# One order for every chunk of ScalarE and GpSimd, group means a chunk earlier, and other places for loads, stores and input statistics

## The chip, the cores and the metric

The kernel runs on one core of a Trainium2 chip. Its five engines run side by side and meet only at semaphores: TensorE (PE in the profile), VectorE (DVE), ScalarE (ACT), GpSimd (POOL), and SyncE (SP), which here only issues DMAs. The metric is the device time of one execution in microseconds (us). Three runs of the kernel before took 4111.73, 4111.97 and 4114.0 us; the median is 4111.97.

## The reference

x has 16 images of 512 channels and 64 x 64 pixels, fp32. Cut to what matters:

```python
# layer 0
g = group_norm(x)                                  # 32 groups of 16 channels, over 16 x 64 x 64 values
gs = [sum_c(g * shift(g, di, dj)) for di in -2..2 for dj in -2..2]     # 25 local correlations
gs = gs / sqrt(sum(gs * gs) + 1e-6)
y = x + relu(W @ concat(g, gs) + bias)             # 1x1 convolution, 537 -> 512
# layer 1
v = group_norm(y)
s = relu(w2 @ relu(w1 @ mean_hw(v) + b1) + b2)     # one number for each image and channel
q = clip(floor(s), 0, 5)
out = y + (s - q) * maxpool[q + 1](v) + (q + 1 - s) * maxpool[q](v) + v   # pools of 1, 3, ..., 13
```

## The kernel before, in words

The program has two phases. The first, some 2500 us long, makes y; the second takes each plane (one channel of one image) of y from memory and pools it. The change touches the first phase alone.

**Tiling.** An image is kept in SBUF as 128 partitions x 4 channel tiles x 4096 pixels, in one of two halves of the arena by the parity of its number. It is worked on in eight chunks of eight rows (512 pixels), numbered 0 to 7 here as in the code, so that "the fourth chunk" is c = 3. `STATS_AT` is 4. Images are numbered 0 to 15. Image 0, image 14 and image 15 are written out in the program; images 1 to 13 are passes of a hardware loop (`Fori`) on VectorE and SyncE (on GpSimd and ScalarE the loop goes to 14; TensorE's holds seven images and runs twice).

**What one chunk costs each engine, in its order:**

- TensorE: `picks` (L1245, gathers the correlations of this chunk from the masked products), two `gram` steps of the next chunk (L1198, products of pixel pairs), `tail` (L1278, the descriptor's part of the convolution of the previous chunk), `norm` (L1268), the two other `gram` steps, then four convolution outputs (L1221 to L1223, 48 matmuls) with `turn_blocks` (L1259) after the first. PSUM banks 4 and 5 hold the gram products in turn: gram step 2 can start only when VectorE has masked step 0.
- VectorE: four `mask` instructions (L791), one for each gram step, with `descriptor` (L833, L837) after the second, `y_stats` (L803, statistics of y for layer 1: the first output after the third mask, three after the fourth), and `wide_rows` (L812 to L827, six maxima of each pixel with its neighbours in the row, of the chunk before). `x_stats` (L741, four instructions) takes the statistics of one chunk of a coming image. In most chunks it stands ahead of the masks.
- ScalarE: `normalise` (L580, L582) of the chunk three ahead, Square (L613), Sqrt (L617), four `conv_out` (L594), `after` (L601).
- GpSimd: `low_parts` (L438, the rounding rest of the fp16 numbers), `residual` (L447, adds the convolution to x in place), `halves` (L457, L459).
- SyncE: `regroup` (12 DMAs of 8 KB that lay the descriptor out for `tail`), `store_wide` (1 MB, the maxima), `store` (2 MB, a quarter image of y), `load` (2 MB, a quarter of the image two ahead, once the same quarter of y is stored).

A chunk of an engine that waits holds up all that is behind it in its queue.

**Group means.** Once per image, the statistics of all eight chunks of the next image are put together: `group_sums` (L751, four instructions on VectorE), `group_average` (L1286, a TensorE matmul into bank N), `group_spreads` (L758 to L764), `group_spread` (L1290, a matmul), `group_root` (L565, ScalarE), `group_values` (L769 to L781). All of these are in chunk 4. TensorE issues `group_spread` last in that chunk; VectorE comes to `group_spreads` only after the maxima. Since the scale is there only at the chunk's end, ScalarE and GpSimd take chunk 5 in another order than all others (`soon`): everything of the coming image's chunk 0 stands behind `conv_out` and `residual`.

```python
if c == STATS_AT and not last and n == 0:      # TensorE, L1315
    group_average(i + 1)
if c == STATS_AT and not last:                 # TensorE, L1317
    group_spread(i + 1)
if c < 5 and left >= 1:                        # VectorE, L862: ahead of the masks
    x_stats(i + 1, c + 2 if c < 4 else CH - 1)
```

At the end of the phase, SyncE stores the last quarter of y and then the maxima of chunks 6 and 7. `wide_rows` of a chunk waits at L819 until the maxima of the chunk before have been stored, since there is one buffer for them.

## Time and profile before

| | |
|---|---|
| median of three runs | 4111.97 us |
| profiled execution, its own time | 4115.68 us |
| its span | 4113.9 us |
| mean granted TensorE clock | 0.915 |
| PE busy | 3403.6 us (83%) |
| DVE busy | 3392.5 us (82%) |
| ACT busy | 1971.2 us (48%) |
| POOL busy | 2080.1 us (51%) |
| packets' time, queue q1 (all of SyncE's DMAs) | 29.2% of 16 engines |

The span begins with the first instruction and ends with the last; the execution's own time is 1.8 us longer. The view of slices cuts the span into 40 equal parts of 102.8 us; a digit 9 is a part in which the engine is busy for 90% or more. In rows of single instructions, or of runs of like ones, the first number is the start, the second the duration, both in us; in brackets stands how long the engine was idle just before and what ended that. "issue" means that nothing the profile shows was waited for. Where the text says "+4.7", it means 4.7 us after the chunk's first `picks` matmul (L1245) on TensorE, which is taken as the start of the chunk.

### The profile page before, as it was taken

The numbers are of one execution on the slowest core, as the hardware profiler recorded it, in microseconds if no ns is written. First come the engines' busy times: TensorE is split into PE (matmuls) and PEld (weight loads), VectorE is DVE, ScalarE is ACT, GpSimd is POOL, SyncE is SP. The second block draws the span as 40 slices with busy tenths as digits, with TensorE's granted clock in tenths as the row PEclk, the third lists the DMA queues.
The fourth block names the chain that finished last, engine by engine and source line by source line (L and its number), as shares of the span: only waits on it lengthen the run. The fifth ranks groups of instructions, "written<-read, shape, count | busy, mean of one in ns | idle before, by whom it ended". The sixth has DMA issues, their size and how long they took to land. (4 is left out here: it accounts for less than half of the span.)

```text
span 4113.9 us, 83924 instructions
## 1 busy us (share of the span) xinstructions
PE 3403.6 (83%) x28232; PEld 1926.1 (47%) x28233; DVE 3392.5 (82%) x3619; ACT 1971.2 (48%) x3219; POOL 2080.1 (51%) x1564
## 2 busy tenths in 40 slices
PE   5999999999999999999999996465666666877665
PEld 3665665565655655665655664122222222333222
DVE  6877777777777777777777766899999999999997
ACT  4544545545545545445545540334444445554566
POOL 4555555555546546556555551345455544454443
PEclk9999999999999999999999996677888888998888
DMA  5454444454445445454454334464565666864466
GB/s 194 162 187 162 167 173 171 169 176 165 160 168 183 160 172 179 161 175 175 167 175 169 129 121 85 172 235 182 226 246 229 265 257 236 338 271 169 182 250 242
DMA packets 251672, 782.36 MB, mean 190 GB/s; under 512 B 97433, under 2 KB 97433, under 8 KB 229273
## 3 DMA queue, kind: packets, MB, share of 16 engines
q1 hardware_dynamic: 219600, 417.47, 29.2%
q0 software_dynamic: 31568, 358.89, 22.2%
q8 instruction: 228, 3.74, 0.4%
q14 instruction: 276, 2.26, 0.2%
HBM read 421.55 MB, written 409.08 MB: 202 GB/s over the span
## 5 line engine op out<-in xcount | busy, mean ns | idle before, releaser
L1041 DVE TENSOR_TENSOR arena<-arena 128x2048 f32<-128x2048 f32 (+8 forms) x635 | 1454.8, 2319 | 57.2 <-DMA arena<-wide_planes,arena 13.8
L438 POOL TENSOR_TENSOR arena<-arena 128x512 f16<-128x512 f32 x512 | 652.4, 1279 | 883.8 <-ACT arena L582 883.5
L1395 PE MATMUL psum<-arena 128*128 128x512 f32 x896 | 532.8, 680 | 465.2 <-issue 313.7
L1198 PE MATMUL psum<-arena 128*128 128x256 f16 (+1 forms) x6344 | 731.1, 274 | 81.5 <-DVE arena L791 61.0
L1221 PE MATMUL psum<-arena 128*128 128x512 f16 x2048 | 777.3, 380 | 1.0 <-ACT arena L594 1.0
L1222 PE MATMUL psum<-arena 128*128 128x512 f16 x2048 | 777.0, 379 | 0.0
L1223 PE MATMUL psum<-arena 128*128 128x512 f16 x2048 | 776.9, 379 | 0.0
L447 POOL TENSOR_TENSOR arena<-arena 128x512 f32 (+1 forms) x512 | 639.6, 1270 | 226.6 <-ACT arena L594 221.7
L580 ACT ACTIVATE arena<-arena,gbias,grstd 128x512 f32 (+1 forms) x512 | 413.7, 808 | 637.3 <-PE psum L1223 527.6
L1198 PEld LDWEIGHTS psum<-arena 128*128 128x128 f16 x6344 | 597.4, 100 | 175.2 <-DVE arena L791 68.5
L1397 PE MATMUL psum<-arena 128*128 128x512 f32 x1072 | 601.6, 659 | 57.0 <-ACT psum L667 47.9
L681 ACT ACTIVATE arena<-psum 128x512 f32<-128x512 f32 x536 | 314.2, 599 | 689.6 <-PE psum L1397 680.4
L803 DVE BATCH_NORM_STATS2 bny<-arena 128x6 f32 (+1 forms) x512 | 351.4, 690 | 266.6 <-POOL arena L447 262.1
L530 POOL DMA_INDIRECT out<-arena x67 | 183.9, 2745 | 747.3 <-issue 747.3
L1395 PEld LDWEIGHTS psum<-arena 128*128 128x128 f32 x896 | 188.4, 217 | 725.2 <-issue 546.3
L594 ACT ACTIVATE arena<-psum,bias_sb 128x512 f32<-128x512 f32 x512 | 337.2, 684 | 219.7 <-POOL arena L447 207.4
L582 ACT ACTIVATE arena<-arena,gbias,grstd 128x512 f16 (+1 forms) x512 | 409.4, 800 | 0.0
L667 ACT ACTIVATE psum<-arena 128x512 f32<-128x512 f32 x536 | 383.1, 766 | 48.6 <-ACT arena L681 47.5
L1397 PEld LDWEIGHTS psum<-arena 128*128 128x128 f32 x1072 | 230.2, 216 | 371.3 <-issue 307.8
L791 DVE TENSOR_TENSOR arena<-psum,cst 128x256 f32<-128x256 f32 x496 | 280.6, 589 | 108.4 <-PE psum L1198 108.3
L741 DVE BATCH_NORM_STATS2 bnx<-arena 128x6 f32 (+1 forms) x512 | 315.1, 680 | 29.5 <-issue 20.7
L1223 PEld LDWEIGHTS psum<-arena 128*128 128x128 f16 x2048 | 200.3, 98 | 241.9 <-issue 0.3
(151 smaller groups left out, 3085.8 us busy)
## 6 DMA issues: line engine op xcount, KB each, us to landing
arena<-in_x SPq DMA_DIRECT2D x64, 2048.0 KB, 13.2
wide_planes<-arena SPq DMA_DIRECT2D x128, 1024.0 KB, 9.3
y_planes<-arena SPq DMA_DIRECT2D x64, 2048.0 KB, 7.8
arena<-arena SPq DMA_DIRECT2D x1536, 8.0 KB, 1.8
arena<-wide_planes,arena POOLq DMA_INDIRECT x69, 11.6
arena<-plane_records,arena POOLq DMA_INDIRECT x67, 7.7
arena<-y_planes,arena POOLq DMA_INDIRECT x67, 9.8
out<-arena POOLq DMA_INDIRECT x67, 9.2
```

Of the source, the lines that this page charges most:

```text
L438: pool.tensor_tensor(gl[:, ct, slot], g32[:, ct % 2, :], gh[:, ct, slot], ALU.subtract).then_inc(s_gl, 1)
L447: pool.tensor_tensor(y, y, relu[:, o % 2, :], ALU.add).then_inc(s_added, 1)
L580: act.activation(g32[:, ct % 2, :], piece, ACT.Identity, bias=gbias[:, ct:ct + 1], scale=grstd[:, ct:ct + 1])
L582: act.activation(gh[:, ct, (c % RING) * CW:(c % RING + 1) * CW], piece, ACT.Identity, bias=gbias[:, ct:ct + 1], scale=grstd[:, ct:ct + 1]) ...
L667: act.activation(psum[:, b, :], bufs[:, u, b * CW:(b + 1) * CW], ACT.Identity, bias=recs_in[:, u, 3:4], scale=recs_in[:, u, 0:1]).then_inc ...
L1041: ins = dve.tensor_tensor(dst, a, b, ALU.max)
L1198: return pe.matmul(dst, w, m, start=(k == 0), stop=(k == nk - 1))
L1221: pe.matmul(dst, h, gh[:, ct, slot], start=(ct == 0), stop=False)
L1222: pe.matmul(dst, h, gl[:, ct, slot], start=False, stop=False)
L1223: last = pe.matmul(dst, l, gh[:, ct, slot], start=False, stop=(ct == CT - 1))
L1395: pe.matmul(dst, diag[:, s, 0, :], small[:, s, b * ROWS:(b + 1) * ROWS, 1:W + 1], start=False, stop=False, skip_group_check=True)
L1397: pe.matmul(dst, diag[:, s, 1, :], big[:, s, b * CW:(b + 1) * CW], start=False, stop=True, skip_group_check=True).then_inc(s_mix, 1)
```

## The change

- VectorE: `x_stats` moves from before the masks to behind the fourth mask, ahead of the last three `y_stats`, by a new function `coming`. Its chunks are other ones: each of chunks 0 to 3 takes one chunk (4 to 7) of the next image, chunk 4 none, chunks 5 and 6 one each (0, 1) and chunk 7 two (2, 3) of the image after.
- Group means: `group_sums` goes to the end of chunk 3 and `group_average` behind its convolutions; `group_spreads` stands at the start of chunk 4, ahead of the masks; `group_spread` behind the second convolution output of chunk 4; `group_values` behind its y statistics, ahead of the maxima.
- TensorE gets waits with which bank N is not written too early: `norm` of chunk 4 waits for the copy of the means (L758 before), `group_spread` for `after` of chunk 5.
- ScalarE and GpSimd take every chunk in one order (`soon` goes).
- SyncE: a chunk is `regroup`, then in odd chunks `load`, then `store_wide` of the chunk before, then in even chunks `store`. Loads go in chunks 3, 5, 7 and in chunk 1 of the next image (before: 4, 6, and 0 and 1 of the next). After the last image the maxima are stored ahead of y.

```diff
@@ SyncE
-            def image(i, prev=True, load_prev=True, load_own=True):
+            def image(i, first=False, left=2):
                 for c in range(CH):
-                    if c >= 2:
-                        store_wide(i, c - 2)
-                    elif prev:
-                        store_wide(i - 1, CH + c - 2)
                     regroup(i, c)
-                    if c == 0 and prev:
-                        store(i - 1, 3)
+                    if c >= 3 and c % 2 and left >= 2:
+                        load(i, c // 2 - 1)
+                    if c == 1 and not first and left >= 1:
+                        load(i - 1, 3)
+                    if c:
+                        store_wide(i, c - 1)
+                    elif not first:
+                        store_wide(i - 1, CH - 1)
                     if c % 2 == 0 and c:
                         store(i, c // 2 - 1)
-                    if c < 2 and load_prev:
-                        load(i - 1, 2 + c)
-                    if c in (4, 6) and load_own:
-                        load(i, c // 2 - 2)
+                    elif c == 0 and not first:
+                        store(i - 1, 3)
...
+            store_wide(B - 1, CH - 1)
             store(B - 1, 3)
-            for c in (CH - 2, CH - 1):
-                store_wide(B - 1, c)
@@ ScalarE (GpSimd likewise)
-                    soon = ahead and c + 3 != CH
-                    if soon:
+                    if ahead:
                         normalise(*ahead, cts=(0, 1), first=first)
...
-                    if ahead and not soon:
-                        normalise(*ahead, cts=(0, 1))
...
-                        normalise(*ahead, cts=(3,) if soon else (2, 3))
+                        normalise(*ahead, cts=(3,))
@@ VectorE
+            def coming(i, c, first, left):
+                todo = []
+                if first and c < 2:
+                    todo += [(1, 2 * c), (1, 2 * c + 1)]
+                if c < 4 and left >= 1:
+                    todo += [(i + 1, c + 4)]
+                if c > 4 and left >= 2:
+                    todo += [(i + 2, c - 5)]
+                if c == CH - 1 and left >= 2:
+                    todo += [(i + 2, 3)]
+                return [lambda at=at: x_stats(*at) for at in todo]
...
-                    sums = [lambda: group_sums(i + 1)] if c == STATS_AT and not last else []
-                    between = [[], sums + [lambda: descriptor(i, c)], res[0:1], res[1:4]]
...
+                    between = [[], [lambda: descriptor(i, c)], res[0:1], coming(i, c, first, left) + res[1:4]]
+                    if c == STATS_AT and not last:
+                        group_spreads(i + 1)
...
+                    if c == STATS_AT - 1 and not last:
+                        group_sums(i + 1)
+                    if c == STATS_AT and not last:
+                        group_values(i + 1)
@@ TensorE
             def norm(i, c, last):
+                if c == STATS_AT and not last:
+                    pe.wait_ge(s_vchain, (i + 1) * STATS_CHAIN + 2)
...
                         if c == STATS_AT and not last and n == 0:
-                            group_average(i + 1)
-                    if c == STATS_AT and not last:
-                        group_spread(i + 1)
+                            group_spread(i + 1)
+                    if c == STATS_AT - 1 and not last:
+                        group_average(i + 1)
```

Three places of the instruction order show what this does. First VectorE at the start of image 14 (chunk 0), where the code is written out; before:

```order
567 L741 BN_STATS bnx<-arena 128x6 x4
568 L791 TENSOR_TENSOR arena<-psum,cst 128x2x16x8 x2
569 L833 RECIPROCAL arena<-arena 128x128
570 L837 TENSOR_TENSOR arena<-psum,arena 128x128
571 L791 TENSOR_TENSOR arena<-psum,cst 128x2x16x8
572 L803 BN_STATS bny<-arena 128x6
573 L791 TENSOR_TENSOR arena<-psum,cst 128x2x16x8
574 L803 BN_STATS bny<-arena 128x6 x3
```

And now (lines of VectorE's helpers have smaller numbers by six: L785 is the mask, L735 `x_stats`, L797 `y_stats`):

```order
565 L785 TENSOR_TENSOR arena<-psum,cst 128x2x16x8 x2
566 L827 RECIPROCAL arena<-arena 128x128
567 L831 TENSOR_TENSOR arena<-psum,arena 128x128
568 L785 TENSOR_TENSOR arena<-psum,cst 128x2x16x8
569 L797 BN_STATS bny<-arena 128x6
570 L785 TENSOR_TENSOR arena<-psum,cst 128x2x16x8
571 L735 BN_STATS bnx<-arena 128x6 x4
572 L797 BN_STATS bny<-arena 128x6 x3
```

The four input statistics stood ahead of the first mask and now stand behind the fourth.

Second, VectorE from the end of chunk 3 to the masks of chunk 4 of the same image, now:

```order
616 L797 BN_STATS bny<-arena 128x6 x3
617 L745 BN_AGGR aggx<-bnx 128x2 x4
618 L806 TENSOR_TENSOR arena<-arena 128x32x31
...
623 L821 TENSOR_TENSOR arena<-arena 128x32x31
624 L752 COPY gm<-psum 128x4
625 L754 TENSOR_TENSOR gd<-aggx,gm 128x4
626 L756 TENSOR_TENSOR gd<-gd 128x4
627 L758 TENSOR_TENSOR gd<-gd,aggx 128x4
628 L785 TENSOR_TENSOR arena<-psum,cst 128x2x16x8 x2
```

Before, the aggregation stood between the second mask and the reciprocal of chunk 4, and the four small instructions behind the maxima of chunk 4, a whole chunk later than here.

Third, SyncE in chunks 6 and 7 of image 0 (L364 `regroup`, L376 `store_wide`, L370 `store`, L384 `load`); before:

```order
20 L364 DMA arena<-arena 32x128 x12
21 L370 DMA y_planes<-arena 128x4x1024
22 L384 DMA arena<-in_x 128x4x1024
23 L376 DMA wide_planes<-arena 128x4x512
24 L364 DMA arena<-arena 32x128 x12
```

And now:

```order
21 L364 DMA arena<-arena 32x128 x12
22 L376 DMA wide_planes<-arena 128x4x512
23 L370 DMA y_planes<-arena 128x4x1024
24 L364 DMA arena<-arena 32x128 x12
25 L384 DMA arena<-in_x 128x4x1024
26 L376 DMA wide_planes<-arena 128x4x512
```

An even chunk issued 2 MB of y and 2 MB of x together, the 1 MB of maxima close behind; now the load goes with the next, odd chunk, and every chunk issues 3 MB.

## Rows read from the trace of the kernel before

**Rows 1.** The page's slices: busy tenths of TensorE.

```profile
PE   5999999999999999999999996465666666877665
```

**Rows 2.** Waits over the whole span: us in total, times, longest.

```profile
PE psum L1198 <- DVE arena L791: 61.0, 39, 5.3
PE psum L1290 <- DVE gd L764: 18.1, 16, 1.2
```

**Rows 3.** TensorE, image 11, chunk 0: start, duration, instruction, idle before.

```profile
1744.52 1.02 PE L1245 MATMUL psum<-arena,cst 128*32 128x24 f32 x96
...
1752.11 4.41 PE L1198 MATMUL psum<-arena 128*128 128x256 f16 x24 [2.67 <-DVE arena L791]
...
1767.24 0.95 PE L1245 MATMUL psum<-arena,cst 128*32 128x32 f32 x88
```

**Rows 4.** Windows: chunk 0 and 6 of image 11, chunk 6 of image 15.

```profile
core 0: us, PE busy (x) PEld busy (x) DVE busy (x) ACT busy (x) POOL busy (x), PEclk, DMA share, GB/s
1744.50:1767.20 22.70, 20.01 (x203) 12.14 (x202) 17.34 (x28) 9.39 (x15) 10.81 (x10) 0.92 0.33 121
1861.20:1879.70 18.50, 17.65 (x202) 10.75 (x201) 15.08 (x23) 9.28 (x15) 10.97 (x11) 1.00 0.18 63
2468.30:2485.70 17.40, 17.40 (x202) 10.75 (x201) 10.98 (x16) 3.67 (x7) 5.62 (x6) 1.00 0.20 70
```

**Rows 5.** TensorE, image 6, chunks 3 and 4.

```profile
1031.20 1.03 PE L1245 MATMUL psum<-arena,cst 128*32 128x32 f32 x96
...
1035.94 2.78 PE L1198 MATMUL psum<-arena 128*128 128x256 f16 x24
...
1049.45 1.03 PE L1245 MATMUL psum<-arena,cst 128*32 128x32 f32 x96
...
1055.02 2.79 PE L1198 MATMUL psum<-arena 128*128 128x256 f16 x24 [0.67 <-DVE arena L791]
...
1063.27 0.28 PE L1286 MATMUL psum<-aggx,cst 128*128 128x4 f32 x2
1069.93 0.39 PE L1290 MATMUL psum<-gd,cst 128*128 128x4 f32 x2 [1.18 <-DVE gd L764]
1070.25 0.95 PE L1245 MATMUL psum<-arena,cst 128*32 128x32 f32 x88
```

**Rows 6.** VectorE, from image 10's last chunk into image 11.

```profile
1742.90 1.23 DVE L819 TENSOR_TENSOR arena<-arena 128x1024 f32<-128x1024 f32 x1 [1.56 <-DMA wide_planes<-arena]
...
1745.90 1.19 DVE L827 TENSOR_TENSOR arena<-arena 128x992 f32<-128x992 f32 x1 [0.22 <-DVE arena L824]
1749.09 2.48 DVE L741 BATCH_NORM_STATS2 bnx<-arena 128x6 f32 x4 [2.00 <-issue]
1751.48 1.01 DVE L791 TENSOR_TENSOR arena<-psum,cst 128x256 f32<-128x256 f32 x2
```

**Rows 7.** VectorE, image 6, chunk 3 and the first mask of chunk 5.

```profile
1039.60 0.57 DVE L791 TENSOR_TENSOR arena<-psum,cst 128x256 f32<-128x256 f32 x1
...
1043.40 0.69 DVE L803 BATCH_NORM_STATS2 bny<-arena 128x6 f32 x1 [0.53 <-POOL arena L447]
...
1046.38 1.18 DVE L812 TENSOR_TENSOR arena<-arena 128x992 f32 x1
...
1050.90 1.19 DVE L827 TENSOR_TENSOR arena<-arena 128x992 f32<-128x992 f32 x1 [0.22 <-DVE arena L824]
...
1072.79 0.59 DVE L791 TENSOR_TENSOR arena<-psum,cst 128x256 f32<-128x256 f32 x1 [0.97 <-PE psum L1198]
```

**Rows 8.** Loads: landing of all 56 (line L384), and SyncE in image 11.

```profile
DMA to landing us min/median/max: 9.4/13.2/15.0
...
1785.34 0.40 SPq L384 DMA_DIRECT2D arena<-in_x  x1
```

**Rows 9.** VectorE, the last maxima of the phase.

```profile
2517.32 1.23 DVE L819 TENSOR_TENSOR arena<-arena 128x1024 f32<-128x1024 f32 x1 [8.18 <-DMA wide_planes<-arena]
```

**Rows 10.** GpSimd and VectorE, image 6, chunk 4.

```profile
1062.95 1.80 POOL L438 TENSOR_TENSOR arena<-arena 128x512 f16<-128x512 f32 x1 [1.20 <-ACT arena L582]
...
1063.65 1.22 DVE L814 TENSOR_TENSOR arena<-arena 128x64 f32 x1
```

More of the change, by code:

```diff
@@ L413, in second_layer_weights @@
                 sp.dma_start(b2_sb, b2.rearrange("(t p) -> p t", p=P), allow_slow_non_contiguous=True).then_inc(s_w12, 16)
-            image(0, prev=False, load_prev=False)
+            image(0, first=True)
             with sp.Fori(1, B - 2) as i:
                 image(i)
-            image(B - 2, load_own=False)
-            image(B - 1, load_prev=False, load_own=False)
+            image(B - 2, left=1)
+            image(B - 1, left=0)
+            store_wide(B - 1, CH - 1)
             store(B - 1, 3)
-            for c in (CH - 2, CH - 1):
-                store_wide(B - 1, c)
             sp.wait_ge(s_recs, 1)
@@ L473, in image @@
                     if ahead:
-                        low_parts(*ahead, cts=(3,) if soon else range(CT))
+                        low_parts(*ahead, cts=(3,))
             for c in range(3):
@@ L608, in image @@
                     ahead = (i, c + 3) if c + 3 < CH else None if last else (i + 1, c + 3 - CH)
-                    soon = ahead and c + 3 != CH
-                    if soon:
+                    if ahead:
                         normalise(*ahead, cts=(0, 1), first=first)
@@ L613, in image @@
                     act.activation(sq, psum[:, BANK_A, 0:QW], ACT.Square).then_inc(s_sq, 1)
-                    if soon:
+                    if ahead:
                         normalise(*ahead, cts=(2,))
@@ L856, in image @@
                         res = [lambda o=o: y_stats(i - 1, CH - 1, o) for o in range(CT)]
-                    sums = [lambda: group_sums(i + 1)] if c == STATS_AT and not last else []
-                    between = [[], sums + [lambda: descriptor(i, c)], res[0:1], res[1:4]]
-                    if c == 0 and first:
-                        x_stats(1, 0)
-                        x_stats(1, 1)
-                    if c < 5 and left >= 1:
-                        x_stats(i + 1, c + 2 if c < 4 else CH - 1)
-                    elif c > 5 and left >= 2:
-                        x_stats(i + 2, c - 6)
+                    between = [[], [lambda: descriptor(i, c)], res[0:1], coming(i, c, first, left) + res[1:4]]
+                    if c == STATS_AT and not last:
+                        group_spreads(i + 1)
                     if c + 1 < CH:
@@ L875, in image @@
                         keep_stats(i - 1)
-                    if c == 3 and left >= 1:
-                        x_stats(i + 1, CH - 2)
+                    if c == STATS_AT - 1 and not last:
+                        group_sums(i + 1)
+                    if c == STATS_AT and not last:
+                        group_values(i + 1)
                     if c > 0:
@@ L881, in image @@
                         wide_rows(i - 1, CH - 1)
-                    if c == STATS_AT and not last:
-                        group_spreads(i + 1)
-                        group_values(i + 1)
             def keep_stats(i):
@@ L1289, in group_spread @@
                 pe.wait_ge(s_xagg, 2 * i + 2)
+                if not (isinstance(i, int) and i == 0):
+                    pe.wait_ge(s_after, (i - 1) * CH + STATS_AT + 2)
                 pe.matmul(psum[:, BANK_N, CT:2 * CT], gavg, gd[:, :], start=True, stop=True).then_inc(s_gavg, 1)
@@ L1315, in image @@
                         if c == STATS_AT and not last and n == 0:
-                            group_average(i + 1)
-                    if c == STATS_AT and not last:
-                        group_spread(i + 1)
+                            group_spread(i + 1)
+                    if c == STATS_AT - 1 and not last:
+                        group_average(i + 1)
             pe.wait_ge(s_const, 32)
```

4 lines of the change are left out of this document (2 added, 2 removed).

## The prediction

> **What bounds the kernel now.** I read the slices first. TensorE stands at 9 in slices 2 to 24 and below it after [rows 1]: the first phase, to about 2500 us, is TensorE's, and the change lies wholly in it. So the only question is where TensorE pauses there. Second the table of waits. Two rows matter: it waited 61.0 us in 39 pieces for VectorE's masks, and 18.1 us in 16 pieces for VectorE before the spread matmul [rows 2]. Third I laid the starts of all 128 chunks on TensorE side by side. An ordinary chunk takes 18.25 us (1031.20 to 1049.45) [rows 5], and 77 of them agree with it within 0.2. Three chunks of every image don't:
>
> - Chunk 0: 22.72 us in image 11 (1744.52 to 1767.24) [rows 3]. In the 13 images 2 to 14 it lies between 21.96 and 25.84, in sum 307.9, which is 70.7 over 13 x 18.25. In image 11, 2.67 of the excess is the wait itself; another 1.8 follows from the clock, for the 24 gram matmuls after the wait take 4.41 us and not 2.78 [rows 3, 5], and the window's granted clock is 0.92, a mean of the 2.4 GHz level and some time at 1.2 [rows 4]. A wait of 0.67 had no such sequel: 2.79 [rows 5].
> - Chunk 4: 20.80 us (1049.45 to 1070.25) [rows 5], the same within 0.05 in images 1 to 13; 2.55 over. That is the late mask (gram step 2 starts at +5.57 where the ordinary one starts at +4.74: 0.83), the average matmul (0.2), the wait of 1.18 before L1290, and its 0.32.
> - Chunk 6: 18.50 where the last image, in which VectorE has little to do, takes 17.40 [rows 4] (it is shorter than the others since an image's last row pair has less to multiply). By the chunk starts the least of images 0 to 14 is 17.49, and the excess over it sums to 10.8 us.
>
> **Why VectorE is late.** Gram step 2 starts 0.63 after the first mask does (1751.48, 1752.11) [rows 3, 6], so the mask must start by +4.74 - 0.63 = +4.1. In chunk 0 it started at +6.96. Back from there [rows 6]: 2.4 of input statistics ahead of it; 2.00 of "issue", which stands at this place in the twelve images 2 to 13, where VectorE's loop turns (3.19 from the start of L827 to the next instruction); and a wait of 1.56 for a store of maxima. SyncE has just issued 5 MB at once.
>
> **The change, part by part.** Own times first, sum at the end.
>
> 1. Input statistics behind the fourth mask. An ordinary chunk: fourth mask ends at +8.97 (1039.60 + 0.57), four input statistics 2.47 to +11.4, three y statistics. The last of these waits for GpSimd's sum and could not begin before +12.2 [rows 7], so it ends near +13.3. The maxima take 5.64 (4.52 from L812 to L827, and 1.12) [rows 7]: VectorE is free at +18.9, that is +0.7 to +1.2 of the next chunk if GpSimd is in its way for a moment. The first mask can't start before its gram step is there, +2.54 (1072.79 against 1070.25) [rows 5, 7]. Room 1.3 to 1.8 before that, and 1.6 more until TensorE feels it. So ordinary chunks stay at 18.25; chunk 6 falls to 17.49: **10.8 gained.**
>
> 2. Chunk 0. Chunk 7 now takes two sets of input statistics. 8.97 + 4.85 = 13.8, three y statistics (0.62 apart when nothing holds them) 15.7, start of L827 4.52 later, +20.2; 3.19 for the loop's turn: mask at +23.4 - 18.25 = +5.1. TensorE's gram step 2 starts at 5.75, 1.0 late, a wait of a size that had no sequel in the clock. The store wait (1.56) goes too: the batch of chunk 6 is now 3 MB, not 5. Eleven images at 1.0, image 8 at 2.1 (TensorE itself turns its loop there and idles 2.06), image 14 at 0 (VectorE has left its loop): 13.1 of the 70.7 remain. **57.6 gained.** From both sides: nothing remains beyond image 8 if VectorE is 1.0 earlier (11 more), and if it is 1 later the wait is 2 and a sequel like that of rows 3 (1.8) comes: 2.8 x 12 = 34 less.
>
> 3. Group means. `group_sums` adds 1.1 to VectorE in chunk 3, `group_spreads` 0.8 before the masks of chunk 4: free at about +2.9, under +4.1. TensorE reaches `group_average` at +18.0 of chunk 3; the sums are there since about +14.5. It reaches `group_spread` at about +13, the differences being there since +3, and ScalarE's `after`, the new wait, ends at +11.2. ScalarE's root then holds only `group_values` (VectorE waits until +13.7 instead of +12.9, seven small instructions, free at +2.3 of chunk 5). Nothing waits long; the two matmuls' 0.5 stays. 13 x (2.55 - 0.5) = 26.7, and in images 0 and 14, whose chunk 4 took 19.46 and 19.84, 1.9. **28.6 gained.** Bounds: up to 0.5 x 15 more if the matmuls were hidden, and 1.18 x 15 less if the wait only changed its place.
>
> 4. The last maxima. L819 waited 8.18 for a store queued behind y's last 2 MB [rows 9]; all of VectorE's sorting, and with it phase two, hangs behind. Now that store is issued some 7 us earlier, before y, and the wait goes: **8.2 gained**, at least 4 if the store lands late.
>
> 5. Small: image 1's odd waits, 0.5 gained. Image 0's chunk 1 takes three sets of input statistics; its maxima end 1.4 too late for chunk 2: **1.4 lost.**
>
> 6. One order on ScalarE and GpSimd: chunk 5 cost TensorE nothing before (18.25 in most images), so nothing by itself; the cover is the 6 us that ScalarE idles in a chunk. Through it GpSimd's late run in chunk 5 goes, which slowed the maxima there; that is in item 1.
>
> 7. SyncE. The wait that can arise: quarter 2 of the next image is read at +9 of chunk 0, quarter 3 at +9 of chunk 2; their loads go out at the end of chunks 7 and 1. In the trace the load at 1785.34, in the same place behind `regroup` of chunk 1, starts at 0.15 before the end of that chunk and is one of those that land in 9.4 to 10.7; the median of 13.2 and the 15.0 are those issued together with 2 MB of y [rows 8]. So it lands at about +9.2. Behind it wait the last y statistics, the maxima and, a chunk later, the masks; with 1.6 + 1.3 of room a delay of half a us costs nothing.
>
> Sum: 57.6 + 28.6 + 10.8 + 8.2 + 0.5 - 1.4 = 104.3. The profiled execution took 4115.7 by its own time: 4011.4. The median of the runs lies 3.7 below it, so 4007.7; I say **4008**.
>
> **A rule that speaks against it.** One GpSimd difference of 1.80 and VectorE's tiny L814 of 1.22 (0.27 elsewhere) lie over each other [rows 10]: each waits for the other, about 0.95 for VectorE. The Trainium skill ("SBUF — State Buffer", section "SBUF: two separate sides") says why: VectorE instructions with two SBUF inputs and GpSimd's share a pair of ports under an exclusive lock, and the later one blocks for the whole of the other. By that rule the maxima, moved some 0.5 us in every chunk, can fall on other GpSimd instructions than before, and in chunk 0 L827 would meet GpSimd's first. One more collision there would make the sum 11 smaller (4019); my sum takes none.
>
> **Rivals.**
> - *The pause at the image's start keeps most of its size.* For: both sets of statistics in chunk 7 and the 2.00 of the loop's turn are in one line now. Against: they add up to +5.1, not to the +6.1 at which the sequel in the clock may come. Price 34: 4042, with chunk 0 at 21 us.
> - *The loads come too late (slower than before).* If a load of quarter 2 or 3 lands L after issue, VectorE is free for the masks at L - 8.9 of the chunk after (issue -0.6, statistics 2.47, y 1.85, maxima 5.64, less 18.25). TensorE feels it from L = 13.0. At 15 (the longest seen) it loses 2.0 and 1.8 of clock, 3.8 in two chunks of 14 images: 106, all the gain. At 16.5 it loses 6 each time, 168: 4176. Against: only 3 MB is under way where 5 MB made 15.
> - *The change doesn't do what it says in chunk 4.* The waits on TensorE's `group_spread` or `norm` bind because VectorE is late: 1.2 x 15 = 18 less, 4026.
>
> **Chances.** Forecast, 0.70. Pause kept, 0.17. Chunk 4 waits, 0.06. Late loads 0.04, of which 0.03 slower. Something that takes all back unseen, 0.03. The range: down to 3994 (item 2's 11 and a little of item 3), up to 4046 (the first rival and a little). This kernel's measurement can tell 0.2%, 8 us. Faster 0.93 (the first three cases), same 0.04, slower 0.03.
>
> **What would show it.** Right: chunk starts on TensorE 18.2 apart but for chunk 0 (near 19.2), 3 and 4 (18.4 to 18.6) and 6 (17.5); waits of L1198 for the mask sum to 15 us or less, the wait before the spread matmul to nearly none; the first mask of chunk 0 at +5; gram steps of 2.8 everywhere; no wait on the last L813. Wrong: `x_stats` idle on a DMA for more than 3 us, gram steps of 4 us and more, or a sum of mask waits above 30.

## The result, and the profile after

The changed kernel takes 4063.26 us (median of four runs, 4060.86 to 4066.45), beside 4112.99 for the kernel before: a ratio of 0.988 (95% interval 0.986 to 0.989), 49.7 us faster. I had said 4008, and 3994 to 4046. The sign was right; half of the gain isn't there.

The profiled execution took 4064.64 us, its span 4062.7. I read it in the order in which I read the one before. First TensorE's row of the page's slices, which answers to [rows 1]. It reads almost the same: the 9s end where they did, and a pause of some us in an image doesn't show in a slice of 102. This view is too coarse for the question.

```profile
PE   5999999999999999999999995455666667876775
```

Then the table of waits (us in total, times, longest), against [rows 2]. Line numbers of the helpers have moved: the mask is L785, the spread matmul L1294, the last maxima instruction L821.

```profile
PE psum L1198 <- DVE arena L785: 43.5, 13, 4.3
PE psum L1294 <- DVE gd L758: 0.9, 1, 0.9
```

The wait before the spread matmul is gone but for the first. The wait for masks fell only from 61.0 to 43.5, where I had said 15 or less, and it is now in 13 pieces and not 39: eleven of 3 to 4.3 us, one an image, and two short ones (1.09 in image 8, 1.73 in image 0). The chunk starts on TensorE say where (sums over images 0 to 14, us):

| chunk | before | after | gained | forecast |
|---|---|---|---|---|
| 0, images 2 to 14 | 307.95 | 305.28 | 2.7 | 57.6 |
| 3 and 4 | 583.9 | 551.6 | 32.3 | 28.6 |
| 5 | 278.7 | 274.0 | 4.7 | 0 |
| 6 | 273.15 | 262.45 | 10.7 | 10.8 |
| 2 of image 0 | 18.22 | 20.12 | -1.9 | -1.4 |
| last chunk's start to last maxima | 34.2 | 26.5 | 7.7 | 8.2 |

All but one of my terms came out within 5 us. Chunk 0 did not come: 54.9 us are missing there. All chunks together, with the last maxima, gained 57 us; the stretch from the last maxima to the end took 1594.0 us before and 1599.5 after. In the twelve profiled executions of kernels with the full computation it lay between 1593.7 and 1599.5 in no order that I can tell, so I don't count it. Of the 4.7 us of chunk 5, 4.1 come from images 6 and 13, where it had taken 20.3 us before, with a gram step 1.9 us late.

The kept terms first. TensorE of image 6, chunk 4 (start, duration; to compare with [rows 5]): the average matmul now stands ahead of the chunk, the spread matmul in its middle without a wait, and the chunk takes 18.45 (18.38 in most images) and not 20.80.

```profile
1033.65 0.28 PE L1288 MATMUL psum<-aggx,cst 128*128 128x4 f32 x2
1033.86 1.03 PE L1245 MATMUL psum<-arena,cst 128*32 128x32 f32 x96
...
1046.89 0.28 PE L1294 MATMUL psum<-gd,cst 128*128 128x4 f32 x2
...
1052.31 0.50 PE L1245 MATMUL psum<-arena,cst 128*32 128x32 f32 x34
```

Now image 11's chunk 0 on TensorE, against [rows 3]. It takes 25.40 us. Gram step 2 waits 4.24, and its 24 matmuls then take 5.30 and not 2.79.

```profile
1709.79 1.02 PE L1245 MATMUL psum<-arena,cst 128*32 128x24 f32 x96
1710.81 2.79 PE L1198 MATMUL psum<-arena 128*128 128x256 f16 x24
...
1718.92 5.30 PE L1198 MATMUL psum<-arena 128*128 128x256 f16 x24 [4.24 <-DVE arena L785]
...
1735.19 1.00 PE L1245 MATMUL psum<-arena,cst 128*32 128x32 f32 x94
```

The windows of this chunk and of chunk 6 of the same image answer to [rows 4]: the granted clock is 0.87 in the first (0.92 before), a mean of the 2.4 GHz level and more time at 1.2; chunk 6 has its 17.5.

```profile
1709.80:1735.20 25.40, 21.16 (x205) 12.74 (x205) 15.71 (x27) 9.39 (x15) 11.21 (x10) 0.87 0.40 130
1826.70:1844.20 17.50, 17.50 (x204) 10.78 (x203) 13.27 (x21) 9.32 (x15) 10.21 (x10) 1.00 0.57 188
```

VectorE at the same place, against [rows 6]:

```profile
1708.69 1.23 DVE L813 TENSOR_TENSOR arena<-arena 128x1024 f32<-128x1024 f32 x1 [0.15 <-DVE arena L808]
...
1711.71 1.19 DVE L821 TENSOR_TENSOR arena<-arena 128x992 f32<-128x992 f32 x1 [0.22 <-DVE arena L818]
1718.27 1.03 DVE L785 TENSOR_TENSOR arena<-psum,cst 128x256 f32<-128x256 f32 x2 [5.37 <-issue]
```

The last maxima instruction starts at +1.92, where I had it (20.2 - 18.25 = +1.95), and the store wait is gone. But then VectorE stands for 5.37 us, put down to "issue", where it had stood for 2.00. In the twelve images 2 to 13 this idle time is 4.47 to 5.43 (1.15 to 2.20 before, from the start of L827 to the next instruction 3.16 to 3.44); in image 14, after the loop, the next instruction follows 1.11 after the start of L821. So the time is lost where VectorE's loop turns, and the turn has become 2.5 to 3.4 us longer than the 3.19 of the prediction. The first mask comes at +7.5 to +8.5, not at +5.1.

What is different at that moment stands in SyncE's queue. The 2 MB load of chunk 7 is issued 1.63 us before L821 starts:

```profile
1710.08 0.41 SPq L384 DMA_DIRECT2D arena<-in_x  x1
```

The view of DMA traffic has a queue of kind "instruction". For the kernel before, from the start of chunk 0 of image 11 to VectorE's next instruction (busy tenths of the 16 DMA engines in 40 slices of 0.12 us, then the queues: packets, MB, share):

```profile
DMA  0021000000000000000001000000000389999999
...
q1 hardware_dynamic: 229, 0.38, 21.8%
q14 instruction: 1, 0.01, 0.5%
```

The one packet of kind instruction (8 KB) is the 1 in the middle; by windows of 0.2 us it moves 1.0 to 1.2 us after L827 starts at 1745.90, on idle DMA engines, and VectorE resumes some 2.1 us after it. The same view of the changed kernel, from L821 to the mask:

```profile
DMA  9789999999999999999998997996999699777997
...
q1 hardware_dynamic: 534, 2.03, 93.9%
q8 instruction: 1, 0.02, 1.0%
q14 instruction: 1, 0.01, 0.5%
```

Here the engines are nearly full from end to end; of the 536 packets in this view 469 are of 4 KB, the load's size. By windows of 0.2 us the 8 KB instruction packet (queue q14) moves 4.4 to 4.6 us after L821 starts, and VectorE resumes some 2.1 us after it, as before. It is the packet that comes late. It is so in all twelve images, by the times of the single packets in the traces: before, the 8 KB packet moves 1.09 to 1.35 us after the last maxima instruction starts and VectorE resumes 2.07 to 2.30 us later; in the changed kernel it moves 3.56 to 4.49 after it, and VectorE resumes 2.00 to 2.17 later. The 16 KB packet of q8 isn't VectorE's: with VectorE's loop written out q14 falls from 276 packets to 221 and q8 keeps its 228 (experiment 2); with TensorE's loop written out as well, q8 falls to 221 (experiment 7).

### The profile page after: what moved, and what is told of

It reads as the page before. It is cut to its first block, busy times and chain, and to the rows that moved or that the text cites. A ratio compares the mean times of both kernels' runs of the same rounds, so it can differ in the third digit from the quotient of the medians.

```text
span 4062.7 us, 83954 instructions
## 1 busy us (share of the span) xinstructions
PE 3398.5 (84%) x28232; PEld 1929.0 (47%) x28233; DVE 3302.9 (81%) x3619; ACT 1970.4 (49%) x3219; POOL 2043.7 (50%) x1564
## 4 chain that ended last, share of the span: by engine, by line
PE 62%; DVE 23%; issue 7%; ACT 4%; POOL 1%; DVEq 1%; DMA 1%; ACTq 1%; SPq 0%; POOLq 0%
DVE arena L1041 20%; PE psum L1198 15%; PE psum L1221 10%; PE psum L1222 10%; PE psum L1223 10%; PE psum L1401 6%; PE psum L1399 4%; PE psum L1245 3%; ACT psum L661 3%; PE psum L1280 2%; PE psum L1259 1%; DVE bnx L735 1%; PE psum L1367 1%; DVE bny L797 1%; PE psum L1270 1%
## 5 line engine op out<-in xcount | busy, mean ns | idle before, releaser
L437 POOL TENSOR_TENSOR arena<-arena 128x512 f16<-128x512 f32 x512 | 617.8, 1208 | 1043.8 <-ACT arena L580 1043.5
L1198 PE MATMUL psum<-arena 128*128 128x256 f16 (+1 forms) x6344 | 728.3, 273 | 59.0 <-DVE arena L785 43.5
L785 DVE TENSOR_TENSOR arena<-psum,cst 128x256 f32<-128x256 f32 x496 | 292.0, 593 | 302.0 <-PE psum L1198 242.9
L797 DVE BATCH_NORM_STATS2 bny<-arena 128x6 f32 (+1 forms) x512 | 334.0, 684 | 114.9 <-POOL arena L446 112.5
L735 DVE BATCH_NORM_STATS2 bnx<-arena 128x6 f32 (+1 forms) x512 | 312.3, 676 | 21.9 <-DMA arena<-in_x 21.9
```

The lines of the kernel that those rows point to most:

```text
L437: pool.tensor_tensor(gl[:, ct, slot], g32[:, ct % 2, :], gh[:, ct, slot], ALU.subtract).then_inc(s_gl, 1)
L1198: return pe.matmul(dst, w, m, start=(k == 0), stop=(k == nk - 1))
```

## The experiments

**Theory A:** at the loop's turn VectorE's code is fetched by DMA, and the fetch stands behind the load that the change has put there. **Theory B:** a pass of the loop needs 4.5 to 5.4 us to start whatever the traffic; before, the input statistics ahead of the masks hid half of it. **Theory C:** the first mask waits for something else, data or a port.

**1. The load made small.**

```diff
+                w = 64 if q == 2 else 1024
-                sp.dma_start(xs_quarter(i % 2, q), x_v[..., q * 1024:(q + 1) * 1024]...)
+                sp.dma_start(xs_quarter(i % 2, q)[:, :, 0:w], x_v[..., q * 1024:q * 1024 + w]...)
```

Expected: 

> The changed kernel, but the load of quarter 2 (issued in chunk 7, right before VectorE's loop turns) brings 64 of its 1024 columns; that part of x is left out, all instructions stay. Theory A (at the loop's turn VectorE's code is fetched by DMA, and the fetch queues behind the 2 MB load that is now in flight): the idle time put down to issue after the last L821 falls from 4.5 to 5.4 us to about 2.0, what it was before the change; the first mask of chunk 0 starts near +5.1, chunk 0 takes about 19.3 instead of 24.1, total about 4063 - 12 x 4.8 = 4005 (3995 to 4020). Theory B (a loop pass needs 4.5 to 5.4 us to start whatever the traffic, and x_stats ahead of the mask hid half of it before): no change, 4063 +- 6, issue still above 4.4. Theory C (the first mask waits for data): no change in the gap.

Measured: the idle time at the turn is 1.88 to 2.24, the first mask at +4.95 to +5.34, chunk 0 at 19.15 to 19.52 in the eleven images, its granted clock 1.00, and the last chunk of the phase starts at 2381.5 where it started at 2436.65: 55.2 us earlier, for 57.6 expected. VectorE, image 11:

```profile
1671.47 1.19 DVE L822 TENSOR_TENSOR arena<-arena 128x992 f32<-128x992 f32 x1 [0.22 <-DVE arena L819]
1674.57 1.03 DVE L786 TENSOR_TENSOR arena<-psum,cst 128x256 f32<-128x256 f32 x2 [1.91 <-issue]
```

The total, 4032.7, is 28 above what theory A said. Most of it is in phase two, which took 20 us longer in the profiled execution. How the planes are pooled depends on their values, and part of x is missing here; that this is the cause of the 20 us is an inference. The page's group of VectorE's pooling has more instructions, first the changed kernel, then this one:

```profile
L1041 DVE TENSOR_TENSOR arena<-arena 128x2048 f32<-128x2048 f32 (+8 forms) x635 | 1454.8, 2320 | 62.9 <-DMA arena<-wide_planes,arena 13.8
```

```profile
L1042 DVE TENSOR_TENSOR arena<-arena 128x4096 f32<-128x4096 f32 (+11 forms) x652 | 1477.3, 2295 | 58.9 <-DMA arena<-wide_planes,arena 12.4
```

I had not thought of that when I wrote the total down. B is out by the gap alone, and so is C as it was written down for this run; a wait of the mask for something that the load's traffic holds up is ruled out only by experiment 2.

**2. No turn.**

```diff
-            with dve.Fori(1, B - 2) as i:
+            for i in range(1, B - 2):
```

Expected: 

> The changed kernel with VectorE's loop over images 1 to 13 written out, nothing else; no turn is left on VectorE. Theories A and B: no idle time behind the last L821, chunk 0 at about 18.3 in all images but 8 (TensorE turns its own loop there), 24.1 - 18.3 = 5.8 less in 11 images and some 2 in image 8: total about 3995 to 4000. Theory C (the mask waits for something other than the turn, data or a port): chunk 0 stays at 24, total 4063.

Measured: 3997.36 us (3996.51 to 3998.41). Chunk 0 is 18.24 or 18.25 in images 1 to 14 but for 5 (18.37) and 8, though the load goes out at the same place as in the changed kernel and takes as long; the wait for masks sums to 1.7 us in one piece. Image 8, where TensorE turns its own loop, takes 22.14: the 2 us that I had expected there did not come (21.71 in the changed kernel). VectorE, image 11:

```profile
1663.98 1.20 DVE L821 TENSOR_TENSOR arena<-arena 128x992 f32<-128x992 f32 x1
1665.36 0.60 DVE L785 TENSOR_TENSOR arena<-psum,cst 128x256 f32<-128x256 f32 x1 [0.18 <-PE psum L1198]
```

The whole of the pause was the turn. A smaller thing goes with it: the idle 0.22 us before L816 and L821, which every pass of the loop has [rows 6], is gone too (0.03 to 0.04 is left).

**3. The load behind the turn, loop kept.**

```diff
-                    if c >= 3 and c % 2 and left >= 2:
+                    if c in (3, 5) and left >= 2:
                         load(i, c // 2 - 1)
...
                         store_wide(i, c - 1)
+                    if c == 7 and left >= 2:
+                        load(i, 2)
...
-                if c < 4 and left >= 1:
-                    todo += [(i + 1, c + 4)]
+                if c < 4 and left >= 1:
+                    todo += [(i + 1, k) for k in ((), (4,), (5, 6), (7,))[c]]
```

Expected: 

> The changed kernel, loop kept, but the load of quarter 2 is issued behind the store of the maxima in chunk 7 (so it cannot start before L821 has ended, and the loop turns before its packets), and the input statistics of chunks 4 to 7 of the next image stand in chunks 1, 2, 2, 3 and none in chunk 0. Theory A: the issue idle time falls to 2 to 3 us unless the load is already running when the fetch begins; chunk 0 at about 19.3 to 20, total 4005 to 4015. Theory B: gap as in the changed kernel, total 4063 +- 6. If the quarter came too late now, the wait would stand on L735 for a DMA in chunk 1.

Measured: 4006.77 us (4004.57 to 4008.46), with all of x loaded. Idle at the turn 1.88 to 2.20, chunk 0 at 19.14 to 19.48 in the eleven images, mask waits 10.8 us in 12 pieces. The DMA view from the last maxima instruction to the mask, image 11:

```profile
DMA  0000000000000030800000000000699999999999
...
q1 hardware_dynamic: 178, 0.36, 30.1%
q8 instruction: 1, 0.02, 2.1%
q14 instruction: 1, 0.01, 0.9%
```

The two packets of kind instruction stand alone on idle engines (the 3 is the one of q14, the 8 that of q8). What follows 1 us later are the 2 KB packets of the store of maxima; the load is issued at 1674.95 and its first 4 KB packet moves at 1677.72, when VectorE has long gone on. So it isn't the amount of traffic that matters, but whether it is there in these 2 us.

The total is that of my forecast, 4008, but not by the same sum, so the last few us of the agreement are luck: chunk 0 of images 2 to 14 gained 55.3 and not 57.6 (image 8 took 22.72, where I had 20.35), chunks 3 and 4 32.0 and not 28.6, chunk 5 4.7 and not nothing.

**4. Group means and the old order of ScalarE and GpSimd back**, the rest of the change kept.

```diff
-                    if ahead:
+                    soon = ahead and c + 3 != CH
+                    if soon:
...
-                    if c == STATS_AT - 1 and not last:
-                        group_average(i + 1)
+                    if c == STATS_AT and not last:
+                        group_spread(i + 1)
```

Expected: 

> The changed kernel with group means and the order of ScalarE and GpSimd as before the change; only input statistics, SyncE's order and the last stores stay changed. If the group means gained their 28.6 by themselves: chunk 4 back to about 20.4 to 20.8, chunk 3 at 18.25, total 4063 + 28 = 4091; chunk 6 stays at 17.5 if the place of the input statistics brought that, and goes to 18.5 (10.8 more, 4102) if the order of chunk 5 on ScalarE and GpSimd did. Rival: with the input statistics moved, chunk 4 would have lost most of its excess anyway, total 4063 to 4075.

Measured: 4094.59 us (4091.79 to 4097.04), 31.3 above the changed kernel. TensorE, chunk 4 of image 6, which takes 20.52:

```profile
1044.95 1.03 PE L1247 MATMUL psum<-arena,cst 128*32 128x32 f32 x96
...
1058.02 0.28 PE L1288 MATMUL psum<-aggx,cst 128*128 128x4 f32 x2
1065.16 0.39 PE L1292 MATMUL psum<-gd,cst 128*128 128x4 f32 x2 [1.66 <-DVE gd L762]
1065.47 0.71 PE L1247 MATMUL psum<-arena,cst 128*32 128x32 f32 x60
```

Chunk 6 stays at 17.63, against 18.50 before and 17.50 changed: the place of the input statistics brought 9 of its 11 us. Chunk 5 sums to 277.5, 3.5 of the 4.7 that I had not forecast; so these belong to the group means or the order of the two engines. Which of the two isn't told apart. Chunks 3 and 4 together sum to 579.1, 27.5 more than in the changed kernel, and chunk 0 to 4.7 less.

**5. The kernel before with SyncE's new order alone.** If A holds, this makes the old kernel's turn worse.

```diff
-                    if c >= 2:
-                        store_wide(i, c - 2)
...
                     regroup(i, c)
+                    if c >= 3 and c % 2 and left >= 2:
+                        load(i, c // 2 - 1)
...
+                    if c:
+                        store_wide(i, c - 1)
...
```

Expected: 

> The kernel before with the changed kernel's order on SyncE alone (loads in odd chunks, so one goes out 0.3 us into chunk 0, and maxima stored first). Theory A says that this puts the load beside VectorE's loop turn here too: start of the last L827 to the next instruction 5.7 to 6.6 instead of 3.2, then x_stats 2.4, the first mask of chunk 0 at +8.5 to +10 and not +7.0, chunk 0 at 24.5 to 26 (23.7 before on average), and only the last maxima gain 8: total 4113 + 24 - 8 = 4129 (4110 to 4145). Theory B (a pass needs a fixed start): the gap stays 3.2, the store wait of 1.6 goes, chunk 0 falls to about 22, total 4113 - 20 - 8 = 4085.

Measured: 4089.5 us (4084.48 to 4097.8). The total lies outside the range that I gave for A (4110 to 4145) and near B's 4085, but the gap does not fit B: from the start of the last maxima instruction (L826 here) to the next one it is 3.2 us in four images, 4.3 to 4.7 in four and 6.1 to 6.4 in four. I had placed L826 at +0.7 or later. Its wait for a store is gone, and it starts at -0.03 to -0.08 in each of these images, which is just when the load goes out, and the gap follows from which comes first. Image 6, VectorE and then SyncE:

```profile
963.25 1.19 DVE L826 TENSOR_TENSOR arena<-arena 128x992 f32<-128x992 f32 x1 [0.22 <-DVE arena L823]
969.32 1.88 DVE L740 BATCH_NORM_STATS2 bnx<-arena 128x6 f32 x3 [4.88 <-issue]
```

```profile
962.66 0.41 SPq L384 DMA_DIRECT2D arena<-in_x  x1
```

The load's issue ends at 963.07, 0.18 before L826 starts. In image 8 it ends 1.04 after:

```profile
1272.83 1.19 DVE L826 TENSOR_TENSOR arena<-arena 128x992 f32<-128x992 f32 x1 [0.22 <-DVE arena L823]
1275.99 1.88 DVE L740 BATCH_NORM_STATS2 bnx<-arena 128x6 f32 x3 [1.98 <-issue]
```

```profile
1273.46 0.41 SPq L384 DMA_DIRECT2D arena<-in_x  x1
```

All twelve images in a row:

| end of the load's issue, from the start of L826 | images | start of L826 to the next instruction |
|---|---|---|
| 0.15 to 0.18 before | 2, 6, 9, 13 | 6.07 to 6.40 |
| 0.27 to 0.39 after | 3, 5, 7, 12 | 4.31 to 4.66 |
| 0.79 to 1.04 after | 4, 8, 10, 11 | 3.16 to 3.21 |

One microsecond in SyncE's queue moves VectorE by three. The single packets say why these are the limits. The load's first packet moves 1.06 to 1.08 us after its issue starts (1.51 in image 7), so it comes 0.47 to 0.52 us after the start of L826 in the first row, 0.94 to 1.05 in the second, 1.46 to 1.71 in the third. In the third row the 8 KB packet of q14 moves at 1.09 to 1.11, ahead of the load; in the first it moves at 3.9 to 4.3; in the second it moves at 2.2 to 2.4, or at 1.15 and then takes 1.72 us where it takes 0.4 to 0.5 in the third (image 12). With B all twelve would be alike. This table, not the total, is what decides.

**6. Half the load** (512 columns in the place of the 64 of experiment 1; that half of x is left out).

```diff
-                w = 64 if q == 2 else 1024
+                w = 512 if q == 2 else 1024
```

Expected: 

> The changed kernel, but the load of quarter 2 brings 512 of its 1024 columns (1 MB; that half of x is left out). Phase one only is to be compared, since phase two depends on the values. If the code fetch waits for all that was queued before it, half the load costs half: issue idle 3.2 to 3.5, mask at +6.4, chunk 0 near 21. If it shares the engines with whatever is running, the delay stays as with 2 MB as long as the load runs: issue 4.5 to 5, chunk 0 near 24.

Measured (one run, phase one alone): idle at the turn 2.95 to 4.42, mean 3.5; chunk 0 at 20.2 to 23.4, mean 21.9. And a regularity: the mask starts 6.6 to 7.1 us after the load is issued in all twelve images, though the load goes out anywhere from 0.62 before to 0.68 after the chunk's start. Image 2, load and VectorE:

```profile
347.28 0.41 SPq L385 DMA_DIRECT2D arena<-in_x  x1
```

```profile
354.02 1.04 DVE L786 TENSOR_TENSOR arena<-psum,cst 128x256 f32<-128x256 f32 x2 [3.04 <-issue]
```

With 1 MB the fetch is through only when the load nearly is (its packet moves 2.1 us before the mask, and the load lands 5.4 to 5.7 after its issue in ten images, 6.6 and 6.7 in two). With 2 MB the mask comes 7.0 to 8.8 after the issue, while this load lands at 9.0 to 10.0, so there the fetch gets in before the end. Of the two ways named in the expectation the first fits 1 MB; neither fits both.

**7. Both loops written out**, VectorE's and TensorE's, and image 0's input statistics two sets to a chunk.

```diff
-            with dve.Fori(1, B - 2) as i:
+            for i in range(1, B - 2):
...
-                with pe.Fori(0, (B - 2) // 7) as g:
-                    for e in range(7):
-                        image(g * 7 + (e + 1), False)
+                for i in range(1, B - 1):
+                    image(i, False)
...
+                if first and c < 4:
+                    todo += [(1, 4 + k) for k in ((), (), (0, 1), (2, 3))[c]]
```

Expected: 

> The changed kernel with VectorE's loop and TensorE's loop over images written out, and image 0's input statistics spread two sets to a chunk (none of the third kind in chunk 1). Against the one with VectorE alone written out (3997.4) image 8's chunk 0 falls from 22.1 to 18.3 (TensorE's own turn goes) and image 0's chunk 2 from 20.1 to 18.3: 3997.4 - 3.9 - 1.8 = 3991.7 (3988 to 3996). If written-out code needs fetches that straight running doesn't hide, idle time put down to issue appears at many places on TensorE and the total stays at 3997 or above.

Measured: 3986.06 us (3984.52 to 3988.16), and 3987.11 when it ran again. It is the fastest kernel of this study, 0.969 of the time before (0.967 to 0.970). Chunk 0 takes 18.18 to 18.21 in images 1 to 14. Image 0's chunk 2 is back at 18.22; its chunk 4 now has a late mask, 19.16. An ordinary chunk takes 18.19 and not 18.24, which I had not forecast; 0.05 in some 110 chunks is about half of the 11.3 us against experiment 2. Images 0 and 15, which stand outside TensorE's loop in every kernel here, have ordinary chunks of 18.19 in all of them, so the 0.05 goes with that loop; why stays open. TensorE's image loop has no "issue" row left in the table of waits, and its mask waits are these:

```profile
PE psum L1200 <- DVE arena L785: 1.3, 3, 0.7
```

The written-out code needs no more fetching. The page's rows of the instruction queues, changed kernel, then this one (packets, MB, share):

```profile
q8 instruction: 228, 3.74, 0.4%
q14 instruction: 276, 2.26, 0.2%
```

```profile
q8 instruction: 221, 3.62, 0.4%
q14 instruction: 221, 1.81, 0.1%
```

**8. The kernel before with VectorE's loop written out**, the one line of experiment 2.

Expected: 

> The kernel before with VectorE's loop over images 1 to 13 written out. Its pause at chunk 0 was 1.6 to 3.9 of store wait, 2.0 of turn and 2.4 of input statistics. Without the turn the mask comes 2.1 us earlier, at +4.9 in most images (21 per cent of a us late) and +7.2 in the four with a long store wait: chunk 0 at 19.1 to 20 in eight images and about 22 in four, 2 to 4 us less in twelve: total 4113 - 38 = 4075 (4065 to 4090). Rival: the store wait grows by what the turn gave, since the stores of 5 MB go out at the same time as before: total 4100 to 4113.

Measured: 4063.58 us (4060.59 to 4066.02), a gain of 51.5 where I had expected 38, and the same time as the changed kernel. Chunk 0 sums to 293.4 for 345.2. The store wait did not grow in most images: L827 starts at +0.8 to +1.9 in ten of the twelve, and the next instruction 1.11 later. Image 11:

```profile
1706.54 1.19 DVE L827 TENSOR_TENSOR arena<-arena 128x992 f32<-128x992 f32 x1
1707.65 2.46 DVE L741 BATCH_NORM_STATS2 bnx<-arena 128x6 f32<-128x512 f32 x4
```

Chunk 4 gained 12.4 and chunk 2 lost 9.5 besides; I did not follow these two, and so the total can't be put down to the turn alone, only the 51.8 of chunk 0 can.

**9 and 10. y's last quarter ahead of the last maxima again**, in the changed kernel and in that of experiment 7.

```diff
-            store_wide(B - 1, CH - 1)
             store(B - 1, 3)
+            store_wide(B - 1, CH - 1)
```

Expected: 

> The changed kernel with y's last quarter stored ahead of the last maxima again. The prediction had 8.2 for this: VectorE's last wide_rows waits 8 us for the store and all behind it moves by as much, total 4063.3 + 8.2 = 4071.5. The profiles so far leave a rival: in phase two, counted from the last maxima, the two kernels with the old order took 1594.0 and 1595.1 and the six with the new one 1593.7 to 1599.5 (mean 1597.2), so some 2 to 3 us may be given back: total 4068 to 4069.

Expected: 

> The kernel with both loops written out (3986.06) with y's last quarter stored ahead of the last maxima. Same question in a second kernel: 3986.1 + 8.2 = 3994.3 if all of the wait counts, 3991.5 if 2 to 3 us are given back in phase two. The wait of VectorE on the store should be about 8.2 again.

Measured: 4066.59 us (4059.22 to 4067.19) and 3984.8 (3983.96 to 3985.81): no difference that counts in either. VectorE doesn't wait in either (shown from the second):

```profile
2383.79 1.23 DVE L813 TENSOR_TENSOR arena<-arena 128x1024 f32<-128x1024 f32 x1
```

I had undone the wrong half. The last `wide_rows` waits for the maxima of chunk 6, and the change stores these in chunk 7 already. Where the very last maxima go is worth nothing.

**11 and 12. The maxima of chunk 6 behind y too**, in the kernel of experiment 7, and that kernel again on the same chip.

```diff
-                    if c:
+                    if left == 0 and c == CH - 1:
+                        pass
+                    elif c:
                         store_wide(i, c - 1)
...
-            store_wide(B - 1, CH - 1)
             store(B - 1, 3)
+            store_wide(B - 1, CH - 2)
+            store_wide(B - 1, CH - 1)
```

Expected: 

> The kernel with both loops written out (3986.06), with the maxima of the last two chunks both stored behind y's last quarter, as before the change. The two kernels that stored only the last maxima behind y did not make VectorE wait at all, so the 8.2 belong to the maxima of chunk 6. Here the wait of about 8.2 must be back. If all of it counts: 3986.1 + 7.7 = 3993.8. If phase two gives back some 2 to 3 of it, as its length in the profiles suggests (1594.5 against 1597.0 from the last maxima to the end): 3991.

Expected: 

> The same kernel as the one with both loops written out, again, beside the run above on the same chip, so that 8 us can be told: 3986 +- 2.

Measured: 3995.96 us (3994.06 to 3997.88) against 3987.11 (3983.54 to 3992.89) on the same chip, 8.9 apart, and the wait of [rows 9] is back to the hundredth:

```profile
2394.75 1.23 DVE L816 TENSOR_TENSOR arena<-arena 128x1024 f32<-128x1024 f32 x1 [8.18 <-DMA wide_planes<-arena]
```

All of the wait counts within the noise of such a comparison (some 2 us); nothing shows that phase two gives any back.

## Why the prediction was wrong

- **The bound, and where TensorE pauses: right.** Every gain and every loss of the six rows of the table above is a pause of TensorE in phase one, or the last maxima behind it.
- **Item 2, chunk 0: wrong, and it is the whole error.** Its steps held up to the start of the last maxima instruction (+1.95 by the sum, +1.88 to +1.92 measured). The one that failed is "3.19 for the loop's turn". I took a duration from [rows 6] as a property of the turn. It is a DMA transfer and its latency, measured in the kernel before with every DMA engine idle. The change moved a 2 MB load to 1.0 to 2.1 us ahead of it, and the 3.19 became 5.7 to 6.6. With that the mask comes at +7.5 to +8.5, TensorE waits 3.3 to 4.3 us, and the sequel in the clock that I had priced into a rival (1.8) comes in each of the eleven images, at 1.6 to 3.1. Experiments 1 and 3 give the 3.19 back (3.07 to 3.43; only in image 8 of experiment 3 4.61, where VectorE then waits for TensorE), and with it chunk 0 at 19.1 to 19.5 in the eleven images; experiment 3 takes 4006.8 us. Item 2 was right for a kernel whose load isn't there at the turn.
- **Item 7, SyncE: asked of the load only when it lands, not what it shares the DMA engines with while it runs.** It landed as forecast (median 9.9, up to 11.1), and where that was late VectorE waited, 12.6 us in 15 pieces, without cost to TensorE.

```profile
  DVE bnx L735: 12.6, 15
...
DMA to landing us min/median/max: 9.0/9.9/11.1
```

- **The rival that the pause keeps most of its size** came nearest in place, but with another mechanism and too small a price: 34 where 55 were lost. It rested on VectorE being 1 us late for no named reason. The other two rivals did not happen. The dearest price of the late loads was added up wrongly: at a landing of 16.5 the mask would be 3.5 late, and with 1.8 of clock that is 5.3 and not 6, so 148 and not 168. Nothing else rests on it.
- **Item 1 right** (10.7 for 10.8), though experiment 4 leaves 1.4 of it with the group means or the order. **Item 3** right in size: chunks 3 and 4 gained 32.3 for 28.6, and 27.5 of it goes when experiment 4 takes the group means and the order back. **Item 6** put chunk 5 at nothing because it took 18.25 "in most images"; the 4.7 that came stood in the others. **Item 4 right in size** (8.9 and 7.7 for 8.2); the words "that store is issued before y" named the wrong store.
- **The collisions on the port**: the one that I weighed, the last maxima instruction against GpSimd's first in chunk 0, did not come. L821 takes 1.19 or 1.20 there in all images of the changed kernel. Before, L827 took 1.85 to 2.10 in six of the images 2 to 14 (1.19 or 1.20 in the others), each time with a new L438 of GpSimd starting within it.

The Trainium skill ("Runtime: NRT & Kernel Launch", section "Instruction fetch mechanics") says that a taken branch to a target outside the window of two prefetched pages makes the engine wait for a DMA fetch. The trace agrees that there is such a fetch: one 8 KB instruction packet of q14 before VectorE goes on in each turn of the twelve images (in image 2 of the changed kernel two), 1.9 to 2.2 us of idle time in experiments 1 and 3, where the DMA engines are free, and up to 5.4 beside a load. The same section of the Trainium skill calls the cost of crossing from one block of code to the next mostly hidden; experiments 2, 7 and 8 agree, with no such idle time of VectorE at any image's start.

## What to carry to other kernels

- An engine's idle time put down to "issue" at the head of a hardware loop can be a code fetch. Its packets run on the same DMA engines as the data, so its length in one profile holds only for the traffic of that profile: before moving a large transfer, look at what stands at its new place, the instruction queues among it.
- If the code can be written out, the turn goes altogether (51.8 us of chunk 0 in experiment 8 for one line, as much as the whole change brought); if not, issue large transfers behind the turn and not ahead of it.
- A term for a single step is best tested by a kernel in which only that step is changed: experiment 8 changes one line and would have shown first what the turn was worth.

## What was not expected of the hardware

- The turn's cost is a matter of fractions of a microsecond (experiment 5): a 2 MB load whose issue ends 0.8 us after the start of VectorE's last instruction costs nothing (3.2), one that ends 0.2 us before it costs 3 us (6.1 to 6.4). The changed kernel's, which end 1.0 to 2.1 before it, cost about as much (5.7 to 6.6).
- TensorE's own turn, in image 8, shows 2.0 to 2.6 us of "issue" idle time. In the changed kernel it ends 2.2 us after a load's issue began and is 1.99, with next to no load in experiment 1 it is 2.06. Its fetch comes ahead of the load: in the changed kernel the 16 KB packet of q8 moves at +0.36 of the chunk and the load's first packet at +1.59, and in all nine other kernels with TensorE's loop that packet moves at +0.34 to +0.88.
- Written-out code has less instruction traffic, not more: 221 packets for 276 in queue q14, and 221 for 228 in q8.
- The kernels with VectorE's loop have 0.22 us of idle time before each dependent maxima instruction, the written-out ones 0.03 to 0.04; with what else differs there, the maxima of a chunk are 0.66 us shorter on VectorE (L821 at +1.23 and not +1.89). I saw it; I did not try it by itself.
- A wait of the same length on TensorE doesn't always have the sequel in the clock. In experiment 4 gram step 2 waited 3.48 us in chunk 0 of image 9, its 24 matmuls then took 2.79, the granted clock of the chunk was 1.00 and the chunk took 21.89; in image 11 the wait was 3.45, and the granted clock 0.93 and the chunk 23.53. In experiment 6 a wait of 2.13 (image 9) had no sequel and one of 1.82 (image 2) had one. So the 1.8 of the prediction is a price that comes or doesn't; what decides it is not shown here.
